# Wide attention: probabilities transposed by VectorE in 32x32 blocks, context mixed in four row tiles; five smaller stages rewritten

## The reference, cut to what matters

```
# wide attention (L2_xattn), context (128, 257, 256), 16 heads of 64
q = split_heads(x @ Wq) * 64 ** -0.5
k, v = split_heads(context @ Wkv)               # 257 keys
k, v = concat(null_k, k), concat(null_v, v)     # 258 keys
attn = softmax(q @ k.T)
out = merge_heads(attn @ v) @ Wout
out = (out - mean) * rsqrt(var + 1e-6) * ln_scale + ln_bias

# depool (L0_xattn, L3_xattn)
h = rmsnorm(x, g_res) @ W_in.T + b_in
out = depool(rmsnorm(context, g_init)) + h      # depool: a weighted sum over rows, here one matmul

# product keys (L0_ffn), the part before the search
q = x @ w_q;  q = (q - mean(q)) * rsqrt(var(q) + 1e-5) * gamma + beta;  sim = q @ keys

# quantised FFN (L2_ffn): scale = max|.| / 127 over the whole tensor
quant(t) = round(t / scale(t))
h = gelu((quant(x) @ quant(w1).T + b1) * s_w1 * s_x)
out = (quant(h) @ quant(w2).T + b2) * s_w2 * s_h

# min GRU (L3_attn): elementwise weights, a scan over the 32 tokens
diff = softplus(-f) - softplus(-i);  h_t = sigmoid(-diff) * h_(t-1) + sigmoid(diff) * g(hidden)
```

## Time and profile before

| | |
|---|---|
| median of 3 runs | 4204.57 us (4201.25 to 4205.80) |
| profiled execution | 4206.12 us, its span 4204.2 |
| TensorE / its weight loads busy | 3441.0 / 2940.5 us (82% / 70%) |
| VectorE, ScalarE, GpSimd busy | 2681.9, 1747.6, 1218.8 us |
| DMA | 147.54 MB, mean 35 GB/s |

### The profile page before, as it was taken

One profiled execution on the slowest core, in us unless ns is written; L12 is line 12 of the kernel. 1 busy time (PEld: TensorE's weight loads), 2 busy tenths in 40 slices (PEclk: granted clock), 3 DMA queues, 4 the chain that ended last, 5 costly groups with the idle time before them and its releaser, 6 DMA issues. The chain is left out here.

```text
span 4204.2 us, 82670 instructions
## 1 busy us (share of the span) xinstructions
PE 3441.0 (82%) x26829; PEld 2940.5 (70%) x26829; DVE 2681.9 (64%) x7434; ACT 1747.6 (42%) x4489; POOL 1218.8 (29%) x1674
## 2 busy tenths in 40 slices
PE   3787787888877888797689999999999999872634
PEld 2676777777765666545479999999999999642334
DVE  6673788888866888757235555555555555477667
ACT  1230566666645777664122333233333333232542
POOL 2551666666642333303100000000000000163021
PEclk8895899999988999998679999999999999986666
DMA  3000000000002222200121111111111111172000
GB/s 86 4 0 33 1 0 0 0 0 0 0 13 70 76 76 75 66 1 6 42 45 42 46 51 46 41 49 48 46 41 51 46 46 43 34 118 38 2 0 22
DMA packets 262351, 147.54 MB, mean 35 GB/s; under 512 B 110327, under 2 KB 258763, under 8 KB 261614
## 3 DMA queue, kind: packets, MB, share of 16 engines
q1 hardware_dynamic: 257742, 140.55, 12.6%
q10 hardware_dynamic: 4512, 5.77, 0.7%
HBM read 131.82 MB, written 13.65 MB: 35 GB/s over the span
## 5 line engine op out<-in xcount | busy, mean ns | idle before, releaser
L901 PE MATMUL psum<-L_ffn_share,L_ffn_prob 128*128 128x128 f32 x4096 | 513.7, 285 | 141.7 <-DVE L_ffn_prob L830 141.7
L901 PEld LDWEIGHTS psum<-L_ffn_share,L_ffn_prob 128*128 128x128 f32 x4096 | 494.0, 199 | 173.3 <-DVE L_ffn_prob L830 141.3
L2129 ACT ACTIVATE L_xattn_prob<-psum,L_xattn_nmax 128x258 f32<-128x258 f32 x512 | 239.1, 472 | 675.7 <-DVE L_xattn_nmax L2164 675.7
L725 POOL TENSOR_TENSOR L_ffn_sums<-L_ffn_sims 128x1024 f32<-128x1024 f32 x256 | 485.8, 1912 | 108.5 <-DVE L_ffn_prob L830 108.2
L2241 PE MATMUL psum<-L_xattn_ctxT,L_xattn_q_ctx 128*128 128x257 f32 x2048 | 488.5, 381 | 0.0
L2279 PE MATMUL psum<-L_xattn_probT,L_xattn_ctx 128*128 128x256 f32 x2048 | 484.6, 379 | 1.7 <-DVE L_xattn_probT L2182 1.7
L830 DVE SCALAR_TENSOR_TENSOR L_ffn_prob<-L_ffn_sums,L_ffn_best,psum 128x512 f32<-128x512 f32 x512 | 358.4, 741 | 107.3 <-ACT psum L758 102.9
L2182 DVE COPY L_xattn_probT<-psum 128x512 f32<-128x512 f32 x256 | 177.1, 692 | 391.1 <-PE psum L2265 391.1
L2104 POOL TENSOR_TENSOR L_xattn_z_var<-L_xattn_z_mv,L_xattn_z_eps 128x1 f32<-128x1 f32 x32 | 6.1, 192 | 1398.1 <-DVE L_xattn_z_mv L2196 1365.3
L2241 PEld LDWEIGHTS psum<-L_xattn_ctxT,L_xattn_q_ctx 128*128 128x128 f32 x2048 | 370.6, 191 | 48.3
L2279 PEld LDWEIGHTS psum<-L_xattn_probT,L_xattn_ctx 128*128 128x128 f32 x2048 | 370.1, 190 | 42.2 <-ACT L_xattn_lastT L2140 2.2
(11 more groups left out here) (432 smaller groups left out, 6590.4 us busy)
## 6 DMA issues: line engine op xcount, KB each, us to landing
L_xattn_ctxT<-ctx_T_dram SPq DMA_DIRECT2D x128, 257.0 KB, 2.8
L_xattn_ctx<-ctx_dram SPq DMA_DIRECT2D x128, 256.0 KB, 3.0
L_xattn_k_all<-ctx_T_dram SPq DMA_DIRECT2D x128, 128.5 KB, 2.1
L_xattn_v_all<-ctx_dram SPq DMA_DIRECT2D x128, 128.0 KB, 2.3
L_attn_qkv_scratch<-L_attn_qkv SPq DMA_DIRECT2D x24, 256.0 KB, 2.8
L_attn_rows<-L_attn_qkv_scratch SPq DMA_DIRECT2D x24, 256.0 KB, 5.3
start_raw<-ctx_dram ACTq DMA_DIRECT2D x16, 256.0 KB, 12.2
start_plug_all<-plug_scratch SPq DMA_DIRECT2D x1, 2048.0 KB, 7.2
```

The lines of the kernel that those rows point to most:

```text
L725: nc.gpsimd.tensor_tensor(sums[:, h % RING, :, :], sx, sy, ALU.add).then_inc(summed, 1)
L901: last = nc.tensor.matmul(pair(2 * s)[:, c * P:(c + 1) * P], prob[:, h % RING, c * P:(c + 1) * P], share[:, h % RING, :], start=(h == 0 an ...
L2129: ins = nc.scalar.activation(prob[:, s, g, :], scores(s)[:, g, :], ACT.Exp, bias=nmax[:, s, g:g + 1], accum_out=total[:, s, g:g + 1])
```

## The change

In wide attention the work goes by sequences rather than by units. VectorE transposes the scaled probabilities by itself, in blocks of 32x32: key 32k + r goes to partition r, and each head lands in one of four groups of 32 partitions (r = head modulo 4). The mix then has 32 rows for each matmul: 8 chunks of 32 keys, four row tiles, each with its own 32 partitions of `ctx` and its own PSUM bank. For that `ctx` is loaded four times, once to each group of partitions. The q of a tile is made in 16 pieces of two matmuls, over three banks. The tail's probabilities go through DRAM. Cut to its core:

```diff
-    ctx = sb("ctx", [P, BT, 2, CD])
+    ctx = sb("ctx", [P, BT, KB, CD])                    # KB = 8 chunks of 32 keys
+    probT = sb("probT", [P, 2, KB, G, SEQ])
-    TURNED, MIX, Q = core.psum[:, 4, :], core.psum[:, 5, :], core.psum[:, 6, :]
+    mix_bank = lambda r: core.psum[:, 4 + r, 0:2 * P]
+    q_bank = lambda k: core.psum[:, 5 + k % 4 % 3, 2 * P:4 * P]
 # SP
-            for dst, src in ((ctxT[:, b, :, :], dram["ctx_T"][ds(seq, 1), :, :].rearrange("a (k c) m -> c (a k) m", c=P)),
-                             (ctx[:, b, :, :], row[0:2 * P, :].rearrange("(k m) c -> m k c", m=P))):
-                sp.dma_start(dst, src).then_inc(ctx_in[b], 16)
+            sp.dma_start(ctxT[:, b, :, :], ...).then_inc(ctx_in[b], 16)
+            for r in range(G):
+                sp.dma_start(ctx[32 * r:32 * r + 32, b, :, :],
+                             row[0:2 * P, :].rearrange("(k m) c -> m k c", m=32)).then_inc(ctx_in[b], 16)
+            sp.dma_start(last_dram, lastT[:, p, :, :].rearrange("p b n -> p (b n)")).then_inc(last_out, 16)
+            sp.wait_ge(last_out, (t + 1) * 16)
 # VectorE, for each half s of the sequence's heads
+            if s == 0:
+                dve.wait_ge(mixed, n - 1 + BT)
+            nc.vector.transpose(probT[:, b % 2, :, 2 * s:2 * s + 2, :].rearrange("p k g n -> p k g n"),
+                                prob[:, s, :, 0:2 * P].rearrange("p g (k m) -> p g k m", m=32)).then_inc(turned, 1)
+            if s == 1:
+                nc.vector.transpose(lastT[:, p, b, :], tail[:, :]).then_inc(lastT_done, 1)
 # VectorE, order for each sequence
+                if following:
+                    maxes(*following[0:2], 0)
+                if before and b == 0:
+                    add_up(t)
+                for piece in q_pieces(t, b, p, after):
+                    q_copy(*piece)
+                if following:
+                    turn(*following, 0)
+                    maxes(*following[0:2], 1)
+                    turn(*following, 1)
 # TensorE
-                for g in range(2):
-                    for k in range(2):
-                        nc.tensor.transpose(TURNED[:, ...], prob[:, s, g, k * P:(k + 1) * P], core.c("ident"))
-                nc.tensor.transpose(TURNED_TAIL, tail[:, s, :], core.c("ident")).then_inc(turned, 1)
+        def mix(t, b):
+            pe.wait_ge(turned, 2 * (t * BT + b) + 2)
+            for c in range(2):
+                for k in range(KB):
+                    for r in range(G):
+                        rows = slice(32 * r, 32 * r + 32)
+                        last = nc.tensor.matmul(mix_bank(r)[:, c * P:(c + 1) * P], ctx[rows, b, k, c * P:(c + 1) * P],
+                                                probT[rows, b % 2, k, :, :].rearrange("p g n -> p (g n)"), start=(k == 0),
+                                                stop=(k == KB - 1))
+            last.then_inc(mixed, 1)
 # TensorE, order for each sequence
+                if following:
+                    score(*following, 0, True)
+                if before and b == 0:
+                    output(t - 1)
+                if before or b:
+                    pe.wait_ge(mix_out, t * BT + b)
+                for piece in pieces:
+                    q_piece(*piece[0:2])
+                if following:
+                    score(*following, 1, True)
+                if pieces:
+                    pe.wait_ge(q_out, t * PIECES + 4 * b + PIECES + 8)
+                mix(t, b)
```

```diff
 # quantised_ffn, VectorE, first layer
+                if live(0):
+                    dve.wait_ge(turned, t + 1)
+                    nc.vector.tensor_copy(qT[:, j, 0, :], bank_a(j)[:, 0:P]).then_inc(qT_done, 1)
+                    if j == 1 and live(-W):
+                        round_x(t + W - 1, (k // W + 1) % 2)
 # min_gru, TensorE
+                nc.tensor.matmul(diff_bank(u), diags[:, 0, :], xnT[:, u, :], start=True, stop=False)
+                nc.tensor.matmul(diff_bank(u), diags[:, 1, :], size[:, u % HALF, :], start=False, stop=False)
...
+                nc.tensor.matmul(diff_bank(u), core.c("ident"), soft[:, u % HALF, 0, :], start=False, stop=False)
+                nc.tensor.matmul(diff_bank(u), diags[:, 2, :], soft[:, u % HALF, 1, :], start=False, stop=True).then_inc(diff_done, 1)
```

More of the change, by code:

```diff
@@ L337, in depool_cross @@
         b_in = sb("b_in", [P, D])
[L338 removed]
         g_init = sb("g_init", [P, D])
[L340 to L346, removed]
+        patch = sb("patch", [P, TILES, D])
@@ L377, in _ @@
+            front.pool_rstd(pool, 0, only=tiles(0))
+            front.pool_rstd(pool, 0, only=tiles(1))
+            pool.wait_ge(rows_in, 32)
+            patches(0)
+            patches(1)
+            for g in range(2, GROUPS, 2):
+                front.pool_rstd(pool, 0, only=pair(g))
+                add_bias(g - 2)
+                patches(g)
+                add_bias(g - 1)
+                patches(g + 1)
+            add_bias(GROUPS - 2)
+            add_bias(GROUPS - 1)
         @block.scalar
@@ L378, in _ @@
         def _(act):
[L379 to L383, removed]
+            for g in range(GROUPS):
+                act.wait_ge(front.turned, (g + 1) * S)
+                if g >= 3:
+                    act.wait_ge(out_done, g - 2)
+                nc.scalar.copy(xnT[:, g % 3, :, :], turn_bank(g)).then_inc(xnT_done, 1)
@@ L404, in _ @@
+            dve.wait_ge(w_in, 32)
+            nc.vector.tensor_scalar(w[:, :], w[:, :], g_res[:, :], None, ALU.mult).then_inc(w_done, 1)
+            for g in range(1, GROUPS + 2):
+                if g % 2 and g + 2 < GROUPS:
+                    front.dve_moments(dve, 0, only=pair(g + 1))
+                if g < GROUPS:
+                    front.dve_normalise(dve, 0, only=tiles(g))
+                if g >= 2:
+                    add(g - 2)
         @block.tensor
         def _(pe):
-            pe.sem_inc(out_done, U)
@@ L407, in _, with turn @@
-            pe.sem_inc(added, U)
-            pe.wait_ge(w_done, 1)
[L409 to L419, removed]
+            def turn(g):
+                if g >= 2:
+                    pe.wait_ge(xnT_done, g - 1)
+                for s in range(S):
+                    pe.wait_ge(front.normed, g * S + s + 1)
+                    nc.tensor.transpose(turn_bank(g)[:, s, :], front.xn[:, g * S + s, :],
+                                        core.c("ident")).then_inc(front.turned, 1)
@@ L971, in _ @@
         def _(dve):
[L972 to L977, removed]
+            front.dve_moments(dve, 0, only=chunks[0])
+            for c in range(1, len(chunks)):
+                front.dve_moments(dve, 0, only=chunks[c])
+                front.dve_normalise(dve, 0, only=chunks[c - 1])
+            front.dve_normalise(dve, 0, only=chunks[-1])
             dve.wait_ge(gram_done, 1)
```

1012 lines of the change are left out of this document (539 added, 473 removed).

## The result

The changed kernel takes 4099.65 us (median of 4 runs, 4096.19 to 4107.63) against 4204.57: the ratio is 0.9754 (95% interval 0.9737 to 0.9771), 105 us less. The forecast was 168 us less, 4036. Its direction and its range hold; its sum is 64 us out, and some 53 of that are in one stage.

The account below looks back on a forecast made before the run. TensorE was taken to bound wide attention, and waits in chains of short phases the smaller stages. From 4206.1 us, -16 (wide attention) and -152 (smaller stages) give 4038, less 1.5: 4036; range 3980 to 4095, chance 0.56.

Parts of the forecast that it names:

- Wide attention, -16: Wide attention: TensorE's work per tile goes from 46.6 to 46.1 us, -16 us for 32 tiles.
- two changes of shape: Wide attention: TensorE loses 0.2 us at each change of tiling shape, two a sequence, 1.6 us a tile.
- the rest of the stage is its filling and draining: Wide attention before the change: 32 tiles give 1491 of 1522.7 us; the remainder was put down to filling and draining.
- the small stages: Two depools, query_keys, folded weights and tokens, quantised FFN and min GRU: shorter chains, -152 us in sum.
- Rival 1: Wide attention's mix: row tiles overlap less, 5.5 us a sequence, +190 us, 4226, slower than before; chance 0.17.
- Rivals 2 and 3: Wide attention: VectorE bounds by a 2 us transpose, 4216, chance 0.05; TensorE doesn't overlap tiles at all, 5370, chance 0.01.
- Rival 4: Wide attention without q stall and with cheap shape changes, some more from small stages: 3930 to 3980; chance 0.14.
- the stall: Wide attention's q: the fourth piece waits until VectorE has copied the first, 0.4 us a sequence, 1.7 a tile.
- Rival 5: The five smaller stages give only half of their forecast gain: 4112; chance 0.07.
- Transfers: Wide attention: loading `ctx` four times needs 111 GB/s, DMA share near 0.4, hidden at no cost.
- Depools, -30: Two depools: loop, `depool` copy and wait for weights go, POOL then bounds at 37.5 us; -15 us each.
- Quantised FFN, -33: Quantised FFN: fewer table loads, tiny bias split, peak in chunks; 151 to 118 us, -33.

Follow-up runs that it names:

- the second transpose: Changed kernel with TensorE's wide-attention loop written out, plus VectorE making each 128x512 transpose of the probabilities twice: 4043.61 us, ratio 0.9622.
- the 4002: Changed kernel with TensorE's wide-attention loop written out, plus a fourth bank for the fourth q piece in three of four sequences: 4002.44 us, ratio 0.9516.

## Why the prediction came out as it did

- **Wide attention, -16: wrong by 53, the step that failed.** The terms of the sum hold: score 1.84 (1.74 and a share of the changes), mix 3.78 (3.57 and a share), q 2.18 (2.19), output 7.36 (7.37), 45.9 a tile (46.1). What mix and scores have over their own rates is 0.4 a sequence, as I took for two changes of shape; that the changes are what costs it was not tested. What failed is what I left out: "the rest of the stage is its filling and draining". The sum went by the work of a tile and never asked what the number of instructions does to the loop. It cost 68 us (4099.65 to 4031.43 when written out), and the 4031 that are left are near the 4036 of the sum because its other errors cancel (wide attention 15 us better than forecast, the small stages 15 to 17 worse, the unchanged ones 9 better). That is luck.
- **Rival 1** (row tiles overlap less, 5.5 us) falls: 128 records in 3.78 us. The reasoning against it fits: what a lone set of tiles has beyond its spacing is not paid again in each of 32 rounds. By the Trainium skill's 3.07 for four row tiles (TensorE: Matmul & The Clock Gate, Measured speedup vs the span model) the mix would have 4.7 us; the trace has 3.78, changes of shape included, so the measurement decides against that figure here: 14.3 / 3.78 is 3.8.
- **Rivals 2 and 3** fall by the second transpose (+12 us for 182) and by the 3.78. **Rival 4** (no stall, cheap changes of shape) falls too: the stall was there, 0.40 us, and the 4002 needed both an edit against it and the loop written out. **Rival 5** (4112) is near the measured 4100, but not by its means: the small stages gave 137 of the 152.
- **Transfers**: 112 GB/s (forecast 111), a share of 0.54 (forecast near 0.4), hidden in the steady part. TensorE waits for `ctx` at the start of the stage only, twice, 6.5 us that I hadn't counted.
- **Depools, -30: -14.** I took POOL alone as the bound. A normalise rose from 0.63 to 0.74 us, while POOL's 30 us now fill more of the stage (47 us for 53); in the changed FFN, where POOL has 7.7 us, one takes 0.345. The row of before (0.63) had the warning, and I left VectorE out of the sum. That a normalise is longer the more of POOL's work runs beside it is shown (0.54 and 0.48 with a third less of it, 0.42 with 20 us in 76); why is not.
- **Quantised FFN, -33: -23.** The front is as forecast (30 us to the peaks). TensorE then waits 3.4 us for the biases' way through DRAM, and the layers take 46 and 45 us where I had 43 and 41: the first is bound by TensorE at half clock, 1.37 a tile (forecast 1.35), and ends in a tail; why the second is 4 longer than before wasn't tested.
- **query_keys -32 (-30), weights and tokens -39 (-31), min GRU -30 (-28)**: by the steps given; that each of their parts brought what was said was not tested singly.

## What to carry to other kernels

Count the instructions of a loop's body on each engine, not only their time: when a change multiplies them, look for a standstill at the jump and at the line of instruction transfers, and write the loop out if there is one. Four row tiles cost nearly what one full pass does in a run of 32 rounds (3.78 us for 3.44 here); a tiny one-row matmul between full ones is dear (1.0 us a tile at half clock). Where POOL and VectorE work at the same time, price them together, by a row in which they did. And when an edit in one stage costs more than that stage shows, measure the other stages as well: 23 of 84 us lay elsewhere.

## What the runs showed of the hardware

- A loop body of 1250 TensorE records is kept from turn to turn (no transfer in 1000 us); at 2500 each jump back costs 2 to 4 us, at 2890 about 5 (some 3.2 us of standstill, then a clock of 0.54 for 3.6 us). The same body in a kernel with 32 more matmuls (128 records) ahead of it stood still for 4.0 to 5.4 us a jump. Code without jumps is fetched in time, at 121 transfers of 16 KB in 1000 us; one to three waits of up to 0.7 us are left. VectorE shows the same between 291 and 323 records.
- 128 records of 32 rows and 128 columns, four tiles at once, take 3.78 us: one in 29.5 ns. The four of a round start some 7 ns apart, and the next round 0.112 us after the first.
- A one-row matmul (two records) among full ones costs TensorE at half clock some 0.30 us beyond its columns, and 0.15 on the pair behind it; with a bias in each tile the pair ahead of the next bias had 0.14 more as well.
- VectorE's transpose of 128x512 float32 in 32x32 blocks takes 0.711 us, a copy from PSUM of that size 0.692.
